# The residual moved from VectorE to an accumulating matmul, and the next image's work spread over 16 steps

## What is computed

```python
t = relu(group_norm(d4_1x1(x, w1), gamma, beta, cmid))
wgt = einsum('oi,bighw->boghw', w2, t) + b2
wv = ...                                   # 9 weights per pixel, symmetry, group
xv = d4_1x1(x, w_v)
pats = unfold_patches(xv, 3)               # 9 shifted copies
out = (wv * pats).sum(axis=4)
...
x = x + conv0(gn(x))
x = x + involution(gn(x))
```

## Time and profile before

| | us |
|---|---|
| median of 3 runs | 5191.05 |
| lowest, highest | 5189.61, 5192.18 |
| the profiled execution, its own time | 5195.25 |
| its span, first to last instruction | 5193.5 |

### The profile page before, as it was taken

The page is one execution under the profiler, slowest core; times in us unless marked ns, Lnnn a source line. Parts: engine busy times, 40 slices in busy tenths (PEclk is TensorE's granted clock), DMA queues, the critical chain, the costliest instruction groups (busy, mean ns, idle before and its releaser), DMA issues.

```text
span 5193.5 us, 113938 instructions
## 1 busy us (share of the span) xinstructions
PE 3796.5 (73%) x36988; PEld 1315.4 (25%) x36988; DVE 4670.5 (90%) x8017; ACT 2854.0 (55%) x4642; POOL 4507.4 (87%) x2208
## 2 busy tenths in 40 slices
PE   8999999978766767676858685767676766767642
PEld 3333333322222222222222221222222222222220
DVE  6777777736999999999999999999999999999998
ACT  7999999956444535354545454444454444535421
POOL 5888888835999999999999999999999999999999
PEclk9999999989888888898889798989898988888866
DMA  7999999943333333232324242323232333333221
GB/s 235 257 257 257 257 256 256 247 107 100 105 102 102 99 106 107 92 121 83 119 83 130 83 127 85 120 91 115 91 110 91 110 103 102 99 106 107 82 74 57
DMA packets 872814, 679.40 MB, mean 131 GB/s; under 512 B 560080, under 2 KB 822736, under 8 KB 855888
## 3 DMA queue, kind: packets, MB, share of 16 engines
q1 hardware_dynamic: 872272, 672.72, 44.2%
HBM read 404.15 MB, written 268.44 MB: 130 GB/s over the span
## 4 chain that ended last, share of the span: by engine, by line
POOL 51%; DVE 13%; issue 9%; PE 4%; POOLq 1%; ACT 1%; DMA 0%; DVEq 0%; SPq 0%; ACTq 0%
POOL acc L1027 51%; DVE prod_p L1078 3%; DVE ps L1122 2%; DVE ps L1119 2%; DVE ps L1078 1%; DVE six_t L1043 1%; DVE acc L1125 1%; DVE prod_d L1078 1%; PE ps L722 1%; PE ps L732 1%; PE ps L773 1%; DVE dev_t L1059 1%; POOLq L1024 1%; DMA xr<-x 0%; POOLq L1026 0%
## 5 line engine op out<-in xcount | busy, mean ns | idle before, releaser
L1027 POOL TENSOR_TENSOR acc<-acc,prod_p 128x1024 f32<-128x1024 f32 x1536 | 3645.0, 2373 | 267.6 <-DVE acc L1125 50.4
L1078 DVE TENSOR_TENSOR prod_p<-ps,val 128x1024 f32<-128x1024 f32 x1536 | 1852.5, 1210 | 111.2 <-POOL acc L1027 110.7
L290 PE MATMUL ps<-xn,band 64*64 64x512 f32 x8192 | 949.2, 599 | 22.1 <-issue 13.7
L773 PE MATMUL ps<-t,w 128*32 128x256 f32 x9216 | 614.0, 425 | 435.7 <-ACT t L936 225.5
L760 PE MATMUL ps<-xm,base 128*32 128x256 f32 (+1 forms) x8192 | 636.2, 445 | 166.4 <-ACT val L923 73.7
L732 PE MATMUL ps<-xh,wh 128*32 128x512 f32 x6144 | 706.8, 600 | 49.6 <-ACT val L923 33.7
L1078 DVE TENSOR_TENSOR prod_d<-ps,val 128x512 f32<-128x512 f32 x1024 | 693.1, 677 | 25.7 <-ACT ps L929 24.0
L722 PE MATMUL ps<-xr,base 128*32 128x512 f32 x4096 | 547.1, 659 | 213.3 <-ACT val L923 124.1
L923 ACT ACTIVATE val<-ps 128x512 f32<-128x512 f32 (+1 forms) x640 | 339.8, 555 | 619.5 <-DVE prod_p L1078 418.0
L322 POOL TENSOR_TENSOR x_out<-x_out,x_in 128x512 f32<-128x512 f32 x512 | 636.2, 1275 | 0.0
L250 ACT ACTIVATE x_out<-ps 64x512 f32<-64x512 f32 x1024 | 606.1, 592 | 52.1 <-PE ps L290 31.8
(11 more groups left out here) (73 smaller groups left out, 3180.1 us busy)
## 6 DMA issues: line engine op xcount, KB each, us to landing
x_in<-x SPq DMA_DIRECT2D x128, 1024.0 KB, 7.4
x<-x_out SPq DMA_DIRECT2D x256, 512.0 KB, 5.2
xr<-x SPq DMA_DIRECT2D x512, 256.0 KB, 3.5
acc<-x SPq DMA_DIRECT2D x1024, 128.0 KB, 2.9
out<-acc SPq DMA_DIRECT2D x256, 512.0 KB, 2.7
prod_p<-wsrc SPq DMA_DIRECT2D x1, 384.0 KB, 4.6
w<-w2t SPq DMA_DIRECT2D x1, 288.0 KB, 4.6
shift_m<-shifts SPq DMA_DIRECT2D x1, 256.0 KB, 5.5
```

The source lines that it names most:

```text
L290: mm = nc.tensor.matmul(ps[to:to + H2, 2 * two + t, :], band[rows, v, rows], group(xn[rows, k % N_RING, :], XP, W, v, 2 * two + x), start= ...
L773: mm = nc.tensor.matmul(taps_of(tap)[32 * q:32 * q + 32, :], w2[:, kt, tap * 32:(tap + 1) * 32], t[:, kt, u, q * UPX:(q + 1) * UPX], start ...
L1027: nc.gpsimd.tensor_tensor(acc[:, r, :], acc[:, r, :], prod_p[:, k % P_RING, :], ALU.add).then_inc(p_added, 1)
L1078: return nc.vector.tensor_tensor(dst.rearrange("p (m r w) -> p m r w", m=count, w=W), taps_of(tap).rearrange("p (m r w) -> p m r w", m=1, ...
```

## The change

- In each half granule VectorE's first product (tap 0) goes to PSUM bank 7. TensorE then adds the residual onto it there, by a matmul of `acc` with a 128 x 128 identity (`same`, kept in `base`), without clearing the bank (`start=False`). The add L1119 is gone; the add of `prod_d` (now L1123) waits for `resid_added`. A half has five operations (`OWN = 10`).
- The order of VectorE's work in a half is new: tap 0, a pooled product, tap 1, a pooled product, the add of tap 1, tap 2, the half sum (now L1128). `product` has line L1086. In the second half the two pooled products are 1 and 2; product 0 stands between the halves and product 3 behind the second.
- On TensorE and ScalarE `lead` is gone. Its values, moments and tap weights stand in granules 14 and 15, and the `LATE` weights in granule 0 of the next image. `inverse` and `forward` come ahead of the values, `block_v` and `block_t` behind the second residual, and three of the tables shift by up to two granules. SP loads some chunks a granule earlier.

In `stage_b`, tables:

```diff
-FORWARD_AT = {0: 0, 1: 1, 2: 2, 4: 3, 6: 4, 7: 5, 8: 6, 9: 7}
+FORWARD_AT = {0: 0, 1: 1, 2: 2, 5: 3, 6: 4, 7: 5, 9: 6, 10: 7}
+INVERSE_AT = {2: (0,), 3: (1,), 5: (2,), 6: (3,), 9: (4,), 10: (5,), 11: (6, 7)}
-INVERSE_AT = {1: (0,), 2: (1,), 4: (2,), 5: (3,), 8: (4,), 9: (5,), 11: (6, 7)}
-LOAD_AT = {1: 1, 2: 2, 3: 3, 5: 4, 7: 5, 8: 6, 9: 7}
+LOAD_AT = {0: 1, 1: 2, 2: 3, 5: 4, 6: 5, 7: 6, 9: 7}
...
-    OWN = 12
+    OWN = 10
...
-        if b == 0:
-            return own, i * (OWN * N_GRAN) + OWN * n + 8
+        if b < 2:
+            return own, i * (OWN * N_GRAN) + OWN * n + (7, 9)[b]
```

TensorE:

```diff
+        def add_resid(i, n, half):
+
+            pe.wait_ge(own, i * (OWN * N_GRAN) + OWN * n + OWN // 2 * half + 1)
+            if half == 0:
+                pe.wait_ge(resid_in[n % ACC_RING], i * (64 * N_GRAN // ACC_RING) + 64 * (n // ACC_RING + 1))
+            nc.tensor.matmul(ps[:, D_BANK, :], same, acc[:, n % ACC_RING, half * HALF:(half + 1) * HALF],
+                             start=False, stop=True, skip_group_check=True).then_inc(resid_added, 1)
+
...
             for n in range(N_GRAN):
-                if n > 0 and n % GRANS == 0:
-                    tap_weights(i, n // GRANS, LATE)
+                u = n // GRANS
+                add_resid(i, n, 0)
+                if n % GRANS == 0 and not (begin and n == 0):
+                    tap_weights(i, u, LATE)
+                if more:
+                    for c in INVERSE_AT.get(n, ()):
+                        inverse(i + 1, c)
+                    if n in FORWARD_AT:
+                        forward(i + 1, FORWARD_AT[n])
+                    if n == MOMENTS_AT:
+                        means(i + 1)
+                        pe.wait_ge(xm_edges, EDGES * (i + 2))
+                        values(0)
+                        variances(i + 1)
+                    if n == N_GRAN - 1:
+                        values(1)
                 if n + AHEAD < N_GRAN:
                     values(n + AHEAD)
+                add_resid(i, n, 1)
                 if more:
                     if n in BLOCK_V_AT:
                         block_v(i + 1, BLOCK_V_AT[n])
                     for c in BLOCK_T_AT.get(n, ()):
                         block_t(i + 1, c)
-                    if n in FORWARD_AT:
-                        forward(i + 1, FORWARD_AT[n])
-                    for c in INVERSE_AT.get(n, ()):
-                        inverse(i + 1, c)
+                    if n == N_GRAN - 1:
+                        values(2)
+                        tap_weights(i + 1, 0, EARLY)
                 if n % GRANS == GRANS - 1 and n < N_GRAN - 1:
-                    tap_weights(i, n // GRANS + 1, EARLY)
-            if more:
-                lead(i + 1)
+                    tap_weights(i, u + 1, EARLY)
```

ScalarE's program changes in the same way. VectorE:

```diff
-        def opening(i, n, a, between):
+        def half_sum(i, n, a, between):
...
             if a == 0:
                 tap_wait(i, n, 0)
             if not fresh:
-                dve.wait_ge(own, g - 1)
-            product(n, 1, prod_d[:, 0, :], m0, QM // 2).then_inc(own, 1)
-            if not fresh:
                 dve.wait_ge(own, g)
             product(n, 0, ps[:, D_BANK, :], m0, QM // 2).then_inc(own, 1)
+            between(0)
+            product(n, 1, prod_d[:, 0, :], m0, QM // 2).then_inc(own, 1)
+            between(1)
+            dve.wait_ge(own, g + 2)
+            dve.wait_ge(resid_added, i * (2 * N_GRAN) + 2 * n + a + 1)
+            nc.vector.tensor_tensor(ps[:, D_BANK, :], ps[:, D_BANK, :], prod_d[:, 0, :], ALU.add).then_inc(own, 1)
             if a == 0:
                 tap_wait(i, n, 1)
             product(n, 2, prod_d[:, 1, :], m0, QM // 2).then_inc(own, 1)
-            if a == 0:
-                dve.wait_ge(resid_in[r], i * (64 * N_GRAN // ACC_RING) + 64 * (n // ACC_RING + 1))
-            dve.wait_ge(own, g + 2)
-            nc.vector.tensor_tensor(ps[:, D_BANK, :], ps[:, D_BANK, :], acc[:, r, half], ALU.add).then_inc(own, 1)
-            between(0)
             dve.wait_ge(own, g + 4)
-            nc.vector.tensor_tensor(ps[:, D_BANK, :], ps[:, D_BANK, :], prod_d[:, 0, :], ALU.add).then_inc(own, 1)
-            between(1)
-            dve.wait_ge(own, g + 5)
             nc.vector.tensor_tensor(acc[:, r, half], ps[:, D_BANK, :], prod_d[:, 1, :], ALU.add).then_inc(own, 1)
...
-            opening(i, n, 0, late)
-            if more and n == 14:
+            half_sum(i, n, 0, late)
+            if more and n == MOMENTS_AT:
                 t_spreads(i + 1)
-            opening(i, n, 1, lambda x: pooled(i, n, x))
-            if more and n == 14:
+            pooled(i, n, 0)
+            half_sum(i, n, 1, lambda x: pooled(i, n, 1 + x))
+            if more and n == MOMENTS_AT:
                 t_add_eps(i + 1)
-            pooled(i, n, 2)
+            pooled(i, n, 3)
             if more and n == 5:
                 t_stats(i + 1, 0)
...
-            pooled(i, n, 3)
```

More of the change, by code:

```diff
@@ L491, in stage_b @@
     first_of = base[:, 3 * P:3 * P + 32]
+    same = base[:, 3 * P + 32:4 * P + 32]
     w_term = prod_p[:, 0, 0:2 * 4 * OQ * 16].rearrange("p (b c o) -> p b c o", b=2, c=4)
@@ L531, in order_of_period @@
         for n in range(N_GRAN):
+            if more:
+                for c in INVERSE_AT.get(n, ()):
+                    yield ("inverse", c), MT
+                if n in FORWARD_AT:
+                    yield ("forward", FORWARD_AT[n]), IRR
             if n + AHEAD < N_GRAN:
@@ L538, in order_of_period @@
                     yield ("block_t", c), MT
-                if n in FORWARD_AT:
-                    yield ("forward", FORWARD_AT[n]), IRR
-                for c in INVERSE_AT.get(n, ()):
-                    yield ("inverse", c), MT
     def order_at_first():
@@ L836, in period @@
                         block_t(i + 1, c)
[L837 to L840 removed]
+                    if n == N_GRAN - 1:
+                        values(2)
+                        tap_weights(i + 1, 0, EARLY)
                 if n % GRANS == GRANS - 1 and n < N_GRAN - 1:
[L842 to L846 removed]
+                    tap_weights(i, u + 1, EARLY)
+        period(0, begin=True)
         with pe.Fori(1, B - 1) as i:
@@ L971, in _, with period @@
         relu(0, 2)
-        def period(i, more=True):
+        def period(i, more=True, begin=False):
             Ring.base, Ring.n, Ring.more = i * PERIOD_MM, LEAD_MM, more
@@ L976, in period @@
                 u = n // GRANS
-                if n > 0 and n % GRANS == 0:
+                if n % GRANS == 0 and not (begin and n == 0):
                     tap_bias(i, u, LATE)
+                if more:
+                    for c in INVERSE_AT.get(n, ()):
+                        keep_inverse(i + 1, c)
+                    if n in FORWARD_AT:
+                        keep_forward(i + 1, FORWARD_AT[n])
+                    if n == MOMENTS_AT:
+                        keep_values(i + 1, 0)
+                    if n == N_GRAN - 1:
+                        relu(i + 1, 0)
+                        keep_values(i + 1, 1)
+                if n == 0:
+                    relu(i, 3)
                 if n + AHEAD < N_GRAN:
                     keep_values(i, n + AHEAD)
-                if n == 0:
-                    relu(i, 3)
                 if more:
@@ L987, in period @@
                         keep_block_t(i + 1, c)
-                    if n in FORWARD_AT:
-                        keep_forward(i + 1, FORWARD_AT[n])
-                    for c in INVERSE_AT.get(n, ()):
-                        keep_inverse(i + 1, c)
                     if n == EDGES_AT:
                         edges(i + 1)
+                    if n == N_GRAN - 1:
+                        keep_values(i + 1, 2)
+                        relu(i + 1, 1)
+                        tap_bias(i + 1, 0, EARLY)
+                        relu(i + 1, 2)
                 if n % GRANS == GRANS - 1 and n < N_GRAN - 1:
                     tap_bias(i, u + 1, EARLY)
-            if more:
-                lead(i + 1)
-        period(0)
+        period(0, begin=True)
         with act.Fori(1, B - 1) as i:
```

39 lines of the change are left out of this document (10 added, 29 removed).

## The result

The changed kernel takes 5495.6 us (median of 4, 5495.1 to 5496.1) against 5191.6 for the one before in the same sessions: 1.059 times as long, 95% interval 1.057 to 1.061, or 304 us more. The prediction said 5350, in a range of 5290 to 5405. The direction was right, and so was the mechanism of the largest term.

What follows compares the result with a forecast made beforehand. It took GpSimd, at 98% of its own floor, to bound the kernel. Granule stalls of 160 us plus 1 at image ends, nothing for the residual, added to the median of 5191.05, gave about 5350 us, range 5290 to 5405.

Steps and rivals of the forecast that it cites:

- What bounds the kernel: GpSimd's adds, 2.52 us apart, run at 98% of their floor; relief of VectorE in mid-image is worth nothing.
- Part 2, the ring: Granule order: add 4, product 2, three operations, half sum, five adds close a 15.84 us loop; GpSimd stalls 0.71 each granule.
- Part 4, the image's end: Granules 13 to 15: 6.1 us lost an image against 6.0 before, 1 us over 15 image ends.
- Part 3, the residual: TensorE's residual matmul before VectorE's add: in time, hidden by 2 us at the tightest place, costing nothing.
- plain stall: GpSimd's wait for the half sum at ordinary granule starts: 0.71 us at 225 starts, 160 us.
- Rival 3: TensorE late at the four unit starts, six taps at low clock: 60 to 150 us more, 5410 to 5500; chance 0.07.
- 4.09 us row: Profile row of three TensorE taps, read as the low clock, at which the residual's cover is gone.
- Rival 1: VectorE's relief shows at image ends without a new granule stall: 5100 to 5160 us; chance 0.05.
- rival 2: VectorE sets the pace and its relief gives back all 307 us: 4885 us; chance 0.01.
- rival 4: Granule stall half as long because VectorE's queue overlaps more: 225 x 0.35 = 80 us, 5270; chance 0.05.

Runs made afterwards that it cites:

- early_sum: Changed kernel with pooled products 0 and 1 inside the second half again and 2 and 3 behind it; 5397.8 us, 1.040 times the kernel before.
- residual_first: Changed kernel, second residual ahead of the values, very first ahead of granule 1's values, first three forward chunks and unit 3's relu one granule later; 5355.4 us (1.031).
- vector_resid: Changed kernel without residual matmuls, VectorE adding the residual itself between the tap-1 product and second pooled product of each half; 5420.0 us (1.044).

## Why the prediction was right in part

**What bounds the kernel: right.** GpSimd's pitch is the floor (adds start 2.51 us apart, 2.52 before). VectorE lost 206 busy us and the kernel gained nothing by it in mid-image.

**Part 2, the ring: right, and nearly to the hundredth.** VectorE's rows of one closing half in the changed kernel, and GpSimd's start behind them:

```profile
3003.71 1.23 DVE L1086 TENSOR_TENSOR prod_p<-ps,val 128x1024 f32<-128x1024 f32 x1 [0.71 <-POOL acc L1035]
...
3004.85 0.69 DVE L1123 TENSOR_TENSOR ps<-ps,prod_d 128x512 f32<-128x512 f32 x1
...
3005.45 0.68 DVE L1086 TENSOR_TENSOR prod_d<-ps,val 128x512 f32<-128x512 f32 x1
...
3006.17 0.69 DVE L1128 TENSOR_TENSOR acc<-ps,prod_d 128x512 f32<-128x512 f32 x1
```

Product 2 waits 0.71 us for GpSimd, then come 1.14, 0.60, 0.72, 0.69 and 0.22 until GpSimd starts at 3007.08: 3.37 from the product's start, where the terms of the prediction give 3.34. A granule takes 15.85 us (3022.95 to 3038.80), predicted 15.84. (That the 0.71 of VectorE's wait here is also the size of the stall is chance; the stall is the 0.71 of the table.)

**Part 4, the image's end: wrong by 26 us, in the change's favour.** The prediction had 1 us lost there; granules 14 and 15 of the 15 images gained 25. The term was the chain from the half sum of granule 14 to the next product, taken as 3.08 us. It took 1.30 (3063.24 to 3064.54), since its one operation with two SBUF inputs met the end of a GpSimd add and not its beginning:

```profile
3063.24 0.69 DVE L1128 TENSOR_TENSOR acc<-ps,prod_d 128x512 f32<-128x512 f32 x1
3063.84 0.14 DVE L1065 TENSOR_TENSOR dev_t<-mv_t,ps 128x2 f32<-128x2 f32 x1
3064.02 0.38 DVE L1067 TENSOR_TENSOR dev_t<-dev_t 128x2 f32<-128x2 f32 x1
3064.44 0.16 DVE L1069 TENSOR_TENSOR spread_t<-dev_t,mv_t 128x2 f32<-128x2 f32 x1
3064.54 1.23 DVE L1086 TENSOR_TENSOR prod_p<-ps,val 128x1024 f32<-128x1024 f32 x1
```

0.38 us where the earlier trace rows has 1.95. The prediction named this as a bound and then took the old value. This takes 1.78 us off an image, 27 in all. Granule 15 came out as worked out (1.92 lost, 2.0 predicted).

**Part 3, the residual: this step failed.** "So it is hidden, by 2 us at the tightest place" put the residual at nothing, and it cost 172 us. The whole adds up so: the plain stall 225 x 0.71 = 160, as predicted; the residual 172, predicted 0; the image's ends -25, predicted 1; shorter adds and the gaps between them -6; in all 300. The step rested on a count of at most eight banks between two residuals, done for a plain granule and a unit's start. The count left out:
- granule 0. Late taps, a forward chunk and four banks of values stand between its residuals, with the relu of unit 3 on ScalarE in the midst. It is 12.9 us where about 10 were free. 122.9 us, of which the plain stall is 11. The images at the lower clock have 12 of them;
- the start. The first residual stood behind the values of granules 1 and 2 and VectorE waited 11.3 us for it, then 9.4 for the second. 20.9 us;
- the loop's jump, 2.4 to 2.8 us of TensorE ahead of the first residual of images 2 to 14, a part of the same 122.9;
- granules 6 and 9, 61.6 us against 23 of plain stall. Here the eight banks were counted, but not that the first residual itself comes late behind the statistics, nor the low clock, which has 32 of the 61.6.

Rival 3 (TensorE late, by the taps at the low clock, 5410 to 5500) had the right engine and the wrong place, and that its range holds the measured time is luck: its price was for the taps at the unit starts, and those of granules 4, 8 and 12 show the plain stall alone. What it had of the truth is the low clock, some 44 us at granules 0, 6 and 9. The 4.09 us row that it leans on was not wholly at the low clock: the granted clock over that row was 0.67.

Rival 1 (no new stall) fell with the gap of 0.87, rival 2 (VectorE sets the pace) with the unchanged pitch of GpSimd's adds and the 206 busy us that brought nothing, rival 4 (half the stall) with the mean of 0.71.

## What to carry to other kernels

Where two engines run through a ring of buffers, follow the ring once around and add up its length; a product moved one place ahead of a sum can close a loop that no idle time elsewhere opens again. When work is moved to a third engine in program order, count what stands ahead of it at every step of the loop, at the first pass, at the image's ends and at the loop's jump above all; the plain step, which is the easiest to look at, was the one without trouble. And two causes of a loss must be taken away together: each fix alone (early_sum, residual_first, vector_resid) left half to three quarters of the loss in place, and early_sum and residual_first together gave back the time of the kernel before, and with the jump out of the way 0.3% less.

## What the runs showed of the hardware

At each of the 13 jumps back to the head of its loop TensorE stood idle for 2.4 to 2.8 us in the changed kernel, and the profile shows nothing that it waited for. What it does in that time the trace doesn't say. It was there before the change (2.6 to 3.1 us), where it fell on work that GpSimd did not feel; its gap at granule 0 was the plain 0.14:

```profile
2962.58 2.59 PE L760 MATMUL ps<-xm,base 128*32 128x384 f32 x14 [2.73 <-issue]
```

A residual matmul (128x128 by 512 columns, fp32) took 1.12 us from start to end at a granted clock of 1.00 (2.4 GHz), and 2.07, behind 3.4 us of idle time, at 0.50 (1.2 GHz); the prediction had put 1.0 and 2.0. And a tiny VectorE operation with two SBUF inputs ended with the GpSimd add that it met, in all 15 images within 0.02 us by the trace: the product of `dev_t` took 0.38 us here in the image shown and 1.95 before, `t_scale` 2.07 here and 0.94 before. So its time in one kernel's trace can't be carried over to another kernel.
